# A Flamingo block on one core: a batch's rows loaded earlier, two turned tiles in two banks, first token sums later, kept rows' loads spread, logits through four banks

## The reference, cut to what matters

```python
x = x + tanh(g_xattn[0]) * attention(layernorm(x), ctx)     # 8 batches, 256 tokens, 512 channels
x = x + tanh(g_ffn[0])   * ffn(layernorm(x))

def attention(hidden, ssm):        # 32 query heads, 8 key heads of 16 channels, window 64, ALiBi
    q = concat(ssm, hidden) @ Wq;  k, v = hidden @ Wk, hidden @ Wv;  ssm_k, ssm_v = ssm @ Wsk, ssm @ Wsv
    return softmax(mask(q @ concat(ssm_k, k).T / 4 + alibi)) @ concat(ssm_v, v) @ Wo

def ffn(x):                        # 2048 tokens
    probs = softmax(x @ w_router)                            # 128 experts, top 4
    basis = silu(x @ w_gate) * (x @ w_up)                    # 8 bases of 256
    out = (coefficients(probs) applied to basis) @ w_down
    return out + (silu(x @ shared_w_gate) * (x @ shared_w_up)) @ shared_w_down
```

## Time and profile before

| | us |
|---|---|
| median of 3 runs | 939.5 (937.07 to 941.76) |
| the profiled execution | 937.33 |
| its span | 935.5 |
| TensorE busy | 888.0 (95%) |
| VectorE busy | 571.5 (61%) |
| ScalarE busy | 401.2 (43%) |
| GpSimd busy | 519.2 (55%) |

### The profile page before, as it was taken

How to read it: one execution, slowest core, us unless ns; L and a number is a source line. 1 busy time by engine, 2 the same in 40 slices (tenths; PEclk the granted TensorE clock), 3 DMA queues, 4 the chain that set the end, 5 groups by cost and what they waited for, 6 DMA issues and landing times.

```text
span 935.5 us, 17701 instructions
## 1 busy us (share of the span) xinstructions
PE 888.0 (95%) x6694; PEld 767.0 (82%) x6694; DVE 571.5 (61%) x1107; ACT 401.2 (43%) x838; POOL 519.2 (55%) x562
## 2 busy tenths in 40 slices
PE   7949999999999999898989989999999999999998
PEld 7848999999999998687867866788888888888886
DVE  5736677767676766672224655845656565655657
ACT  5615454545555454554014223344344444444431
POOL 5533343434343431443207998854888788888831
PEclk9979999999999999899999999999999999999999
DMA  7666576676857565990101134431110221211036
GB/s 233 149 146 156 157 200 173 178 197 153 221 143 218 143 173 142 251 311 25 45 1 46 31 116 129 142 125 68 44 70 23 68 69 44 68 51 41 23 113 247
DMA packets 79358, 115.44 MB, mean 123 GB/s; under 512 B 6561, under 2 KB 49314, under 8 KB 78242
## 3 DMA queue, kind: packets, MB, share of 16 engines
q1 hardware_dynamic: 77000, 113.28, 42.6%
q10 hardware_dynamic: 2274, 1.03, 0.5%
HBM read 75.95 MB, written 36.24 MB: 120 GB/s over the span
## 4 chain that ended last, share of the span: by engine, by line
PE 84%; DMA 4%; DVE 3%; POOL 3%; SPq 2%; issue 2%; ACT 1%; POOLq 0%; DVEq 0%; ACTq 0%
PE ps_scores L2004 19%; PE ps_proj L1676 12%; PE ps_scoresT L2004 9%; PE ps_scores L1781 6%; PE ps_scoresT L1802 6%; PE ps_scores L1665 5%; PE ps_o L1816 5%; PE ps_proj L2004 5%; PE ps_proj L1665 5%; PE ps_scoresT L1665 4%; PE ps_proj L1730 4%; SPq L534 1%; DMA q_kept<-second_qT_hi 1%; DMA xn_rows<-in_x 1%; POOL x_normal L757 1%
## 5 line engine op out<-in xcount | busy, mean ns | idle before, releaser
L999 ACT ACTIVATE probsT<-ps_scoresT 128x512 f32<-128x512 f32 (+1 forms) x256 | 137.2, 542 | 149.8 <-PE ps_scoresT L1802 149.4
L1324 DVE TENSOR_REDUCE neg_max<-ps_scores 128x2 f32<-128x384 f32 (+1 forms) x256 | 131.5, 516 | 75.5 <-PE ps_scores L1781 71.2
L1781 PE MATMUL ps_scores<-k_stack,q_stack 114*128 114x192 f32 (+1 forms) x512 | 100.5, 280 | 17.5 <-DVE neg_max L1324 16.7
L1210 ACT ACTIVATE part_sums<-ps_scores 128x512 f32<-128x512 f32 x96 | 57.5, 599 | 131.8 <-PE ps_scores L2004 130.4
L1802 PE MATMUL ps_scoresT<-q_stack,k_stack 116*128 116x256 f32 x448 | 103.8, 303 | 3.7 <-ACT probsT L999 3.1
L1781 PEld LDWEIGHTS ps_scores<-k_stack,q_stack 114*128 114x128 f32 x512 | 82.3, 192 | 28.5 <-issue 14.5
L875 POOL TENSOR_TENSOR w_expert_lo<-w_sums,w_expert_hi 128x256 fp32r<-128x256 f32 x64 | 64.3, 1014 | 45.6 <-ACT w_expert_hi L1130 45.6
L887 POOL TENSOR_TENSOR big<-big,basis 128x512 f32<-128x512 f32 x56 | 77.5, 1403 | 15.5 <-DVE basis L1615 15.5
L739 POOL TENSOR_TENSOR oT_lo<-oT_raw,oT_hi 128x256 fp32r<-128x256 f32 x32 | 23.6, 738 | 111.7 <-ACT oT_hi L1010 111.7
L1802 PEld LDWEIGHTS ps_scoresT<-q_stack,k_stack 116*128 116x128 f32 x448 | 71.5, 194 | 6.1 <-issue 4.0
L733 POOL TENSOR_TENSOR o_normal<-o_blocks,inv_sums 128x128 f32<-128x128 f32 x64 | 25.8, 403 | 90.0 <-DVE inv_sums L1344 90.0
(11 more groups left out here) (276 smaller groups left out, 2556.3 us busy)
## 6 DMA issues: line engine op xcount, KB each, us to landing
k_stack<-k_kept SPq DMA_DIRECT2D x64, 192.0 KB, 5.6
q_stack<-q_kept SPq DMA_DIRECT2D x28, 384.0 KB, 5.5
big<-coeff_rows SPq DMA_DIRECT2D x8, 1024.0 KB, 4.8
q_kept<-qT_hi SPq DMA_DIRECT2D x12, 512.0 KB
xn_rows<-in_x SPq DMA_DIRECT2D x8, 512.0 KB, 5.9
k_kept<-kT_hi SPq DMA_DIRECT2D x16, 256.0 KB
x_rows<-in_x SPq DMA_DIRECT2D x8, 512.0 KB, 5.0
x_kept<-x_rows SPq DMA_DIRECT2D x16, 256.0 KB, 5.0
```

The costliest lines, as they stand in the source:

```text
L999: act.activation(PT[:, g % 2, 2 * j:2 * j + blocks].rearrange("p h f r w -> p (h f r w)"), ST[:, n % 2, 0:blocks].rearrange("p h n -> p (h ...
L1210: act.activation(TP[:, u % 2, j, :], src[:, u % 2, :], ACT.Copy).then_inc(taken, 1)
L1324: dve.tensor_reduce(NM[:, g % 2, 2 * i:2 * i + 2], SA[:, n % 2, :, 0:keys], AX.X, ALU.max, negate=True).then_inc(max_done, 1)
L1781: ins = pe.matmul(SA[:, n % 2, f, 0:2 * (near.stop - near.start)], QS[0:TOP, g, i, f].rearrange("p r w -> p (r w)"), keys[:, near, :].rear ...
```

## The change

Seven edits.

1. `load_x(2)`, batch 2's rows of x, is issued after the stacks of head 2, ahead of head 3's; `load_rows(2)` keeps its place and loads the context alone.
2. `x1_normalise` is cut into its two tiles; for batches 0 to 6 the second follows one slot later, behind `scale_outputs` of that slot.
3. The last batch's two tiles are turned at slots 282 and 283 instead of 286 and 288; the second goes to a bank of `PJ` and waits for `residual(7, 0)` instead of for the first tile's split. The last router product goes from slot 290 to 286, and to the second bank of `PG`, and so waits for the sixth silu; `gate_up` of the tile q = 7 instead of q = 6 waits for the last logits.
4. The 12 loads of kept rows go from every third slot from 226 on to every fourth from 215 on, so that three of them are issued ahead of slot 224; the router's and the first shared weights' loads go from slot 225 to 233.
5. ScalarE splits the shared weights 2 ahead of the silu of q = 7 instead of behind it.
6. The logits are turned through four banks with no wait for each other's copy; a wait for the attention's last turned outputs and maxima is added.
7. `S1_AT` goes from t = 3, 7, 10, 13 to t = 5, 8, 11, 14; VectorE's `sum4_low(0)` and `(1)` go from t = 12 and 15 to 14 and 15.

```diff
--- before.py
+++ after.py
@@ -63,7 +63,7 @@
 SUMS_AT = {8: 0, 10: 1, 12: 2}
-S1_AT = {3: 0, 7: 1, 10: 2, 13: 3}
+S1_AT = {5: 0, 8: 1, 11: 2, 14: 3}
 S4_BY_DVE, S4_OP = 2, {8 + m: divmod(m, 3) for m in range(6)}
@@ -93,7 +93,7 @@
 TANH = 40
-XT_AT = {2 + 3 * m: (m // 2, m % 2) for m in range(2 * SPILLED)}
+XT_AT = {4 * m - 9: (m // 2, m % 2) for m in range(2 * SPILLED)}
 END = B * UNITS
@@ -123,7 +123,7 @@
 def x_turn_slot(b, t):
-    return (69, 72)[t] if b < B - 1 else (62, 64)[t]
+    return (69, 72)[t] if b < B - 1 else (58, 59)[t]
@@ -135,7 +135,7 @@
 TILES_S = [(0, 0), (0, 1), (1, 0), (1, 1), (0, 2), (1, 2), (0, 3), (1, 3)] + [(n, t) for n in (2, 3) for t in range(4)]
-ROUTER_AT = {0: 0, 4: 1, 12: 2, 34: 3}
+ROUTER_AT = {0: 0, 4: 1, 12: 2, 30: 3}
 SHARED_AT = {15: 0, 17: 1, 20: 2, 23: 3, 25: 4, 28: 5}
@@ -361,6 +361,7 @@
     JOBS, TURNS = projections(), turns()
+    LAST_TURN = ("x", B - 1, TB - 1)
     FIRST_BANKS = {("k", 0, 0): POB[:, :, :].rearrange("p h n -> p (h n)")}
@@ -374,6 +375,8 @@
         kind, b, t = job
+        if job == LAST_TURN:
+            return PJ[:, len(JOBS) % 2, :]
         return PJ[:, b, :] if kind == "prep" and b < 2 and t == 1 else PT_
@@ -452,6 +455,9 @@
+    def logits_bank(q):
+        return PJ[:, q, :] if q < 2 else PC[q - 2]
+
     def down_bank(i):
@@ -499,9 +505,13 @@
-        def load_rows(b):
+        def load_x(b):
             sp.wait_ge(prep_t, TB * b)
             sp.dma_start(XN[:], x_t[:, b]).then_inc(x_in, 16)
+
+        def load_rows(b):
+            if b != 2:
+                load_x(b)
             sp.wait_ge(ctx_lo, 2 * b)
@@ -558,6 +568,8 @@
             stack_q_first(g)
+            if g == 2:
+                load_x(2)
             if g == 3:
@@ -605,7 +617,7 @@
             s = n - (END - UNITS)
-            if s == 1:
+            if s == 9:
                 sp.wait_ge(q_kept, 16 * PARTS * (B - 1))
@@ -746,16 +758,15 @@
-        def x1_normalise(b):
+        def x1_normalise(b, t):
             if b >= 1:
...
                 pool.wait_ge(xT_kept, 48 * b)
-            for t in range(TB):
-                n = b * TB + t
-                pool.wait_ge(x1_rt, b + 1)
-                pool.tensor_scalar(X1N[:, t, :], X1[:, t, :], x1_mv[:, n, 0:1], x1_rstd[:, n:n + 1],
-                                   ALU.subtract, ALU.mult).then_inc(x1_n, 1)
+            n = b * TB + t
+            pool.wait_ge(x1_rt, b + 1)
+            pool.tensor_scalar(X1N[:, t, :], X1[:, t, :], x1_mv[:, n, 0:1], x1_rstd[:, n:n + 1],
+                               ALU.subtract, ALU.mult).then_inc(x1_n, 1)
@@ -790,10 +801,13 @@
                 x1_roots(b)
-                x1_normalise(b)
+                x1_normalise(b, 0)
             m = group_due(n, O_TURN)
...
                 scale_outputs(m)
+            b = batch_at(n, lambda b: x1_roots_slot(b) + (1 if b < B - 1 else 0))
+            if b is not None:
+                x1_normalise(b, 1)
             m = group_due(n, O_HIGH)
@@ -1025,7 +1039,7 @@
             act.wait_ge(router_mm, q + 1)
-            act.activation(logitsT[:, q, :], PG[:, q % 2 if q < 3 else 0, :], ACT.Copy).then_inc(logits_out, 1)
+            act.activation(logitsT[:, q, :], PG[:, q % 2, :], ACT.Copy).then_inc(logits_out, 1)
@@ -1141,9 +1155,9 @@
                 shared_hi(1)
-            silu(q)
             if q == 7:
                 split_hi(SHARED + 2, (up_mm, used[0, 3] + 1))
+            silu(q)
             if q == 8:
@@ -1470,7 +1484,7 @@
             dve.wait_ge(logits_t, q + 1)
-            dve.tensor_copy(PR_[:, q * 4:(q + 1) * 4, 0:E], PJ[:, q % 2, :].rearrange("p (t e) -> p t e", e=E)
+            dve.tensor_copy(PR_[:, q * 4:(q + 1) * 4, 0:E], logits_bank(q).rearrange("p (t e) -> p t e", e=E)
                             ).then_inc(logits_in, 1)
@@ -1568,8 +1582,8 @@
                 sum4(*S4_OP[t])
-            if t in (12, 15):
-                sum4_low((t - 12) // 3)
+            if t >= NT - 2:
+                sum4_low(t - (NT - 2))
         for t in range(NT - 2, NT):
@@ -1699,6 +1713,8 @@
                     pe.wait_ge(pj_done, passed("v", 0, 0))
+            elif job == LAST_TURN:
+                pe.wait_ge(pj_done, passed("wo", B - 1, 0))
             elif TURNS[job] >= 1:
@@ -1850,15 +1866,15 @@
                 pe.wait_ge(turn_done, passed("x", B - 1, TB - 1))
-                pe.wait_ge(silu_done, FIRST_TILES - 1)
-            product(PG[:, q % 2 if q < 3 else 0, :], lambda h, c: WR[h][:, c * P:(c + 1) * P], tokens(q), range(HC)
+                pe.wait_ge(silu_done, FIRST_TILES)
+            product(PG[:, q % 2, :], lambda h, c: WR[h][:, c * P:(c + 1) * P], tokens(q), range(HC)
                     ).then_inc(router_mm, 1)
...
                 pe.wait_ge(exp_done, END)
-            if q == FIRST_TILES:
+            if q == FIRST_TILES + 1:
                 pe.wait_ge(logits_out, NG)
@@ -1939,10 +1955,10 @@
                 pe.wait_ge(turn_done, len(TURNS))
-            if q >= 2:
-                pe.wait_ge(logits_in, q - 1)
+                pe.wait_ge(o_turned, GROUPS)
+                pe.wait_ge(nm_out, GROUPS)
             for j in range(4):
-                ins = pe.transpose(PJ[:, q % 2, j * P:(j + 1) * P], logitsT[:, q, j * P:(j + 1) * P], ident[:])
+                ins = pe.transpose(logits_bank(q)[:, j * P:(j + 1) * P], logitsT[:, q, j * P:(j + 1) * P], ident[:])
             ins.then_inc(logits_t, 1)
...
```

## The result

The changed kernel takes 926.7 us (median of 4 runs, 925.14 to 929.94), the kernel before 938.29 in the runs beside it (934.59 to 941.76): a ratio of 0.9882, 95% interval 0.9834 to 0.993. The forecast was 918.8, in a range of 911 to 927: the measured time is inside the range at its upper end, outside the forecast's own 913 to 923. The profiled execution took 927.07, its span is 925.3.

The account below looks back on a forecast made before the run. TensorE, busy 888 of 935.5 us, was taken as the bound, through its waits and slow clock. Terms 4.8 + 4.1 + 0.4 + 4.1 + 2.8 + 3.3 = 19.5 us gave 917.8 to 920.0; 918.8 was taken, range 911 to 927.

Parts of the forecast that it names:

- A: First stacks, slots 16 to 32: loading batch 2's rows earlier ends VectorE's wait for them; 4.8 us won, 3.5 to 7.3.
- C: Slots 223 to 229: normalisation cut in two scales outputs sooner and removes most of TensorE's wait; 4.1 us, at least 2.08.
- D: Kept rows' loads spread, around slots 224 to 255: +0.4 us won, from -3 (three heads late) to +1.5.
- F: Last shared tiles: turning the last batch's tiles earlier, in two banks, removes three waits; 4.1 us, at least 3.55.
- G: Shared tiles: logits without a bank wait and weights 2 split earlier remove 0.67 and 1.69 us waits; 2.8 us, 2.3 to 3.1.
- H: Shared down product: later first sums remove waits at t = 3 to 13, partly lost in unit 0; 3.3 us, 1 to 6.5.
- my mark: Sign at the last batch's maxima: transfers taking 9 us or more would show D negative.
- gains are caught sooner: Rival, all terms: each gain meets its next wait within 2 us; 11 us won, 927 us; chance 22 in 100.
- slower rival: Batch 7, slots 231 to 266: moved loads delay the maxima's transfers, five times 7.0 us; 953 us; chance 2 in 100.
- point of decision: Transfer time of the maxima in batch 7 from which the slower rival decides: 10.6 us.

Follow-up runs that it names:

- A undone: Changed kernel with batch 2's rows loaded at their old place, the moved kept-row loads retained: 931.9 us, ratio 0.9923.
- C undone: Both tiles normalised in one go: changed kernel, 927.43 us; with D undone, 923.85; with old kept-row loads, unit 0 repaired and later split of weights, 918.27.
- D undone: Changed kernel with the kept rows' loads and the router's load back at their old slots: 922.41 us, ratio 0.9819.
- D alone: Kernel before with only the kept rows' loads and the router's load moved to their new slots: 944.63 us, ratio 1.0054.
- H alone: Kernel before with only the later first sums of the shared down product: 937.28 us, ratio 0.9979.

## Why the prediction was off

| term | predicted | shown | by |
|---|---|---|---|
| A | 4.8 (3.5 to 7.3) | 5.2 in medians (3.9 by ratios), 5.5 to 7.3 in traces | A undone; slot 32 |
| C | 4.1 (at least 2.08) | 0.7 to 1.4, inside the intervals; about 3 at its place | C undone, three times |
| D | +0.4 (-3 to +1.5) | -3.6 to -5.5; -4.0 and -4.4 from slot 228 to 252 | D undone, D alone |
| F | 4.1 (at least 3.55) | 4.4 to 5.9 | traces |
| G | 2.8 (2.3 to 3.1) | 3.4 | trace, twice |
| H | 3.3 (1 to 6.5) | 1.2 | H alone; unit 0 |

- **A was right**, by its chain: `keep_q(1)` at 63.26 as foreseen, 13.0 us from its first issue to its landing, slot 32 4.9 us behind. Slot 32 began at 81.12, ahead of the 83 to 85 that I had given, because two surcharges were too much: the landing came at 76.2 instead of 77.2, and slot 30 waited 1.77 us, not 4, and the clock did not fall. (My 84 for slot 32 would also have made A 4.4, not the 4.8 of the sum.)
- **D was wrong in sign, and it is the step that failed.** I wrote that the loads "leave the stretch behind slot 224 by as many bytes as they bring in front of it, where the queue had room". Three loads did move in front of slot 224, at 364.15, 367.12 and 369.40 us, but they landed 6.7, 7.3 and 10.3 us later, so all were still under way when slot 224 began at 369.60. The DMA share rose to 0.84 in the window from 366 to 369 us and to 1.03 behind it. The room lay earlier, with shares of 0.50 and 0.24 from 360 to 364 us, and D did not reach it. Not because of the buffer: the last `v` product is copied out at 355.39. SP takes its queue in order, and in front of the first load stands `stack_q` of slot 214, which waits until the queries of batch 7 are stored (the first line is from SP's list of waits, 350 to 370 us: total us, times, longest; the second from VectorE's timeline):

```profile
SPq L552 <- DMA q_kept<-qT_hi: 6.2, 1, 6.2
...
355.39 0.68 DVE L1322 COPY vT<-ps_proj 128x512 f32<-128x512 f32 x1
```

  No run puts a load ahead of that `stack_q`, so whether the room is of use stays open. What the runs show in place of +0.4 is a loss of 3.6 to 5.5 us.
- **What D's price consists of** I had only the smaller part. I counted late maxima alone. The larger part is the store: in the traces with D its low part is issued 13.8 to 15.5 us behind the start of slot 228, with the old order 8.1 to 12.5. ScalarE waits for it at slot 242 and holds the next maxima. Without C it is nearly all: slots 244 to 248 take 10.98 and 10.58 us with D, 5.3 to 6.7 with the old order. Moving ScalarE's split behind it gave back 3.5 us.
- The Trainium skill (DMA: Bandwidth & Descriptors, Issuing engines are not separate DMA queues) pointed at the maxima's part: I told its rule, that DMAs started by different engines run on the same 16 DMA engines and interleave, and then gave it no weight in the sum. The traces agree in part. The transfer behind slot 231 took 9.5 to 10.4 us in the four traces with D and C and mostly 6.8 to 8.4 with the old order; but it took 10.83 in one with the old order, and 7.91 in both with D and without C. So my mark, 9 us or more for D negative, was passed by luck: it does not tell the kernels with D from those without.
- **C was right at its place and wrong as a term of the end.** The wait at slot 229 went from 2.71 to 0.62 us, slots 228 to 232 took 3.6 us less, as against 4.1. I had asked what is late next for the normalisation only. Late next was what was in flight: the traces with C wait up to 3.9 us for maxima or 2.2 us behind ScalarE in the next slots. I read this so, that the 2.7 us of standing still and the slow clock after it had been time in which transfers landed. My own number said so: a head has 6.7 us at full speed, and the transfer took 7.75.
- **H had the right mechanism**, wait 2.76 for "some 3 us", given back at the clock 4.6 - 2.8 = 1.9 for 1.8. Mis-sized was the gain ahead of it: 5.9 us instead of 7.5, since VectorE's `down_lo` made TensorE wait in six other places, 1.12, 0.17, 0.38, 0.39, 0.34 and 0.36 us, where before there were two of 0.52 and 0.53: 1.7 us more.
- **F and G were right** and a little small, by 0.3 to 1.8 and by 0.6.
- The rival *gains are caught sooner* gave the right time, 927, with the wrong parts: A, F and G lost nothing (5.2, 4.4 and 3.4 against its 3.5, 3.6 and 2.3), while D lost more than the -2 that it had and than my bound of -3. That its time fits is luck. The slower rival's mechanism, maxima behind the moved loads, was there with C, but its point of decision was not reached in the changed kernel: 10.07 us against 10.6, and TensorE stood over 1 us for it once, not five times.

## What to carry to other kernels

Where the DMA engines are full, don't count the stall of a compute engine as time to be won: ask of a removed wait what each load and store in flight will then be late for. Here a wait and the slow clock behind it, 3 us at their place, were worth nothing twenty slots later. Move loads out of such a stretch only to where the windows show the engines idle, where the buffer is free, and where the issuing engine comes to them in its own order; then look at what is queued behind them. A gain with nothing else due behind it (two banks for one, an earlier split) came in full, at 4.4 us or more and 3.4. And before a difference of some us in a stretch is explained, look at other traces with the same code there: here they were up to 3.7 us apart.

## What the hardware showed

- The same transfer of 8 KB behind slot 231 took 6.75 to 10.83 us, at DMA shares of about 1.0. One of 384 KB took 12.2 us, where the median of four in the kernel before (360 to 420 us) was 7.0.
- SP's issue of one transfer took 1.3 to 2.6 us for a run of issues from 379 to 391 us in the changed kernel, at DMA shares of 1.03 to 1.14. Others at such shares took 0.4 to 0.6, so the share alone does not tell it.
- A wait of 3.45 us had the clock at 0.65 over its last 2 us and at 0.50 for 5 us behind it. One of 1.77 us alone had no fall (1.00 up to 84 us); two of 1.11 and 0.81 close together were followed by 0.57 over 4 us.
- Two waits of 1.41 us, 2 us apart, left the clock at 1.00 in one execution and had it at 0.50 to 0.66 for 4 us in two others, 1.5 us of TensorE's time. A short wait has no fixed price.
